# A perceiver layer on one core: outputs by transposes, values of four batches in one visit, and other steps of the cross-attention put elsewhere

## What is computed

```python
q = layernorm(x).reshape(B, 32, 16, 8)            # 16 heads of 8 channels
k = v = ctx.reshape(B, 257, 16, 8)
A = softmax(einsum('blhe,bshe->bhls', q, k) / sqrt(8)) * mask     # mask (32, 257)
out = einsum('bhls,bshd->blhd', A, v)
x = x + transpose(out, (0, 2, 1, 3)).reshape(B, 32, 128)   # heads first
```

## Time and profile before

| | us |
|---|---|
| runs: median of 3 (lowest to highest) | 1053.57 (1051.38 to 1054.31) |
| the profiled execution: its own time | 1050.45 |
| its span, first to last instruction | 1048.7 |
| stage 1: first scores to its last addition | about 20 to 529 |
| mean granted TensorE clock | 0.965 |

### The profile page before, as it was taken

How to read it: one execution, slowest core, us unless ns; L and a number is a source line. 1 busy time by engine, 2 the same in 40 slices (tenths; PEclk the granted TensorE clock), 3 DMA queues, 4 the chain that set the end, 5 groups by cost and what they waited for, 6 DMA issues and landing times. The chain is left out here.

```text
span 1048.7 us, 25999 instructions
## 1 busy us (share of the span) xinstructions
PE 927.9 (88%) x7666; PEld 815.4 (78%) x7666; DVE 840.0 (80%) x2152; ACT 648.9 (62%) x2006; POOL 606.9 (58%) x531
## 2 busy tenths in 40 slices
PE   3959999999999999999948888878899888888983
PEld 2848888888888888888848888778788787878872
DVE  5747787878788787878758887886499999999995
ACT  2626566656666566666536666666477777767674
POOL 4335555655555564556344444443477777877786
PEclk9979999999999999999969998999999999999997
DMA  4021212212221212221400000000000000000000
GB/s 119 25 74 56 58 50 65 55 47 60 55 65 43 65 55 52 56 65 54 142 1 1 0 0 0 0 0 1 1 2 10 5 10 5 10 5 6 9 5 16
DMA packets 48676, 35.34 MB, mean 34 GB/s; under 512 B 3660, under 2 KB 48392, under 8 KB 48648
## 3 DMA queue, kind: packets, MB, share of 16 engines
q1 hardware_dynamic: 48648, 35.00, 12.2%
HBM read 32.88 MB, written 2.10 MB: 33 GB/s over the span
## 5 line engine op out<-in xcount | busy, mean ns | idle before, releaser
L551 ACT ACTIVATE E<-SC,neg_max 128x257 f32<-128x257 f32 x512 | 238.4, 471 | 161.2 <-DVE neg_max L613 161.1
L425 PE MATMUL SC<-Kt,Qbd 128*128 128x257 f32 x1024 | 279.6, 396 | 1.0 <-ACT E L551 0.8
L613 DVE TENSOR_REDUCE neg_max<-SC 128x2 f32<-128x514 f32 x256 | 177.0, 691 | 86.6 <-PE SC L425 75.2
L425 PEld LDWEIGHTS SC<-Kt,Qbd 128*128 128x128 f32 x1024 | 176.9, 193 | 31.4 <-issue 14.1
L301 POOL TENSOR_TENSOR Qbd<-Qt,head_scaled 128x2048 f32<-128x2048 f32 (+2 forms) x33 | 145.1, 4398 | 80.0 <-ACT Qt L541 80.0
L621 DVE TENSOR_TENSOR Et<-ETP,mask_T 128x512 f32<-128x512 f32 x256 | 174.0, 680 | 15.0 <-PE ETP L439 14.9
L439 PE MATMUL ETP<-ident,E 128*128 128x128 f32 x1024 | 156.1, 275 | 0.0
L1371 PE MATMUL PO<-W,hid 128*128 128x128 f32 x1024 | 138.2, 278 | 18.8 <-ACT hid L1412 18.7
L1371 PEld LDWEIGHTS PO<-W,hid 128*128 128x128 f32 x1024 | 131.4, 192 | 29.0 <-issue 21.5
L1436 ACT ACTIVATE Y<-Z,zb,zs 128x128 f32<-128x128 f32 x256 | 111.0, 485 | 60.1 <-DVE zb L1591 60.1
L439 PEld LDWEIGHTS ETP<-ident,E 128*128 128x128 f32 x1024 | 125.3, 142 | 20.5 <-issue 0.4
(11 more groups left out here) (161 smaller groups left out, 1579.1 us busy)
## 6 DMA issues: line engine op xcount, KB each, us to landing
V<-in_ctx_dram SPq DMA_DIRECT2D x64, 256.0 KB, 2.9
last_all<-in_ctx_dram SPq DMA_DIRECT2D x32, 256.0 KB, 5.0
xh<-in_x_dram SPq DMA_DIRECT2D x32, 64.0 KB, 3.7
X<-in_x_dram SPq DMA_DIRECT2D x32, 64.0 KB
out_dram<-Xo SPq DMA_DIRECT2D x64, 32.0 KB, 1.5
W<-in_L_ffn_w_dram SPq DMA_DIRECT2D x1, 1024.0 KB
W<-in_L_ffn_w_dram SPq DMA_DIRECT2D x2, 512.0 KB
last_row<-in_ctx_dram SPq DMA_DIRECT2D x32, 2.0 KB
```

What stands on the lines that cost most here:

```text
L425: i = pe.matmul(SC[s % 2][:, u, 0:S], Qbd[:, h, jj, g:g + HQ, :].rearrange("p q l -> p (q l)"), Kt[:, h, jj, 0:S], start=True, stop=True)
L551: i = act.activation(E[:, h, u0 + u, :], SC[s % 2][:, u, 0:S], ACT.Exp, bias=neg_max[:, s % 2, u:u + 1], accum_out=den[:, h, u0 + u:u0 + u ...
L613: dve.tensor_reduce(neg_max[:, s % 2, :], SC[s % 2][:, :, 0:S], AX.X, ALU.max, negate=True).then_inc(max_sb, 1)
```

## The change

- The four products with `gather_d` become four transposes of `O_m` (128 columns a batch). The head mask falls away at `keep_sums`, which becomes a plain copy on ScalarE behind the exponentials of step 3 (`AV_STEP`). Shares are spread over heads instead (`spread_shares`, new, VectorE, step 3: reciprocal sums times the block mask, `own_p`), and `last_probs` and `own_outputs` multiply by them, 64 and 512 wide. GpSimd multiplies the last row by them in one instruction and then folds: three additions, 512, 256 and 128 wide (`fold` for `add_last`).
- `weigh_values` of four batches in one visit at step 2 of the next half; `Et` holds 16 steps instead of 8. The loads of the context follow: batches 4 and 5 of a tile are loaded with 6 and 7, 0 and 1 with 2 and 3.
- `turn_queries`, `keep_queries` and `place_last` at step 1 instead of 0.
- The second `turn_keys` at step 5 instead of 6 (`keep_keys` at 6), `turn_out` and `own_outputs` at step 4 instead of 5, `turn_tile` at 6 instead of 7.
- The tables are made within tile 0 (steps 3 to 6, in bank `AV`), the two memsets for stage 2 behind the first placing of queries there, and at the start some loads and small instructions change their order.

```diff
+AV_STEP = 3
...
 rden = sb1("rden", [P, HB * NQ])
-Et = sb1("Et", [P, HSTEPS, 2, KT, HQ * L])
+own_p = sb1("own_p", [P, HB * NQ, HQ])
...
+            load_ctx(sp, t, 2)
             load_ctx(sp, t, 3)
...
-        sp.wait_ge(av_ps, TB * t + 2)
-        sp.nop(nofuse=True)
-        load_ctx(sp, t + 1, 0)
...
+        load_ctx(sp, t + 1, 0)
         load_ctx(sp, t + 1, 1)
...
     load_x(sp, 0, 0)
     load_last(sp, 0, 0)
     load_ctx(sp, 0, 0)
+    load_x(sp, 0, 1)
+    load_ctx(sp, 0, 1)
+    load_last(sp, 0, 1)
     for n, src in zip("qkvo", (Wq, Wk, Wv, Wo)):
...
-    load_x(sp, 0, 1)
-    load_ctx(sp, 0, 1)
-    load_last(sp, 0, 1)
...
         m = 2 * t + h
         pool.wait_ge(all_in[h], 16 * (t + 1))
+        pool.wait_ge(p_last, m + 1)
         pool.tensor_tensor(last_x[:, :, :, :],
...
-    def add_last(t, h):
+                           last_p[:, :, :].unsqueeze(3).to_broadcast([P, HB * NQ, HQ, DK]),
+                           ALU.mult).then_inc(o_last, 1)
+
+    def fold(t, h):
 
         m, n = 2 * t + h, HB * NQ
         pool.wait_ge(o_n, m + 1)
         pool.wait_ge(o_last, m + 1)
-        mine = O_n[:, :, n * h:n * (h + 1)].rearrange("p d u -> p u d")
-        pool.tensor_tensor(mine, mine, last_o[:, :, :], ALU.add).then_inc(o_both, 1)
+        pool.tensor_tensor(last_x[:, :, :, :], last_x[:, :, :, :], own_x[:, :, :, :], ALU.add).then_inc(o_sum, 1)
+        pool.wait_ge(o_sum, m + 1)
+        pool.tensor_tensor(pair_x[:, :, :, :], last_x[:, :, 0:2, :], last_x[:, :, 2:4, :], ALU.add).then_inc(o_pair, 1)
+        pool.wait_ge(o_pair, m + 1)
+        if h == 0 and not (isinstance(t, int) and t == 0):
...
+        pool.tensor_tensor(O_n[:, :, n * h:n * (h + 1)].rearrange("p d u -> p u d"),
+                           pair_x[:, :, 0, :], pair_x[:, :, 1, :], ALU.add).then_inc(o_both, 1)
 
     def add_tile(t):
...
+            if fresh and h == 0:
+                pool.memset(Kbd[:, :, :, :], 0.0).then_inc(pool_set2, 1)
+                pool.memset(Vbd[:, :, :], 0.0).then_inc(pool_set2, 1)
             if h == 1 and not fresh:
...
 
     power(0, 0)
-    power(0, 1)
-    pool.wait_ge(dve_set, 1)
-    place_queries(0, 0, 0, 1, q_first)
-    place_queries(0, 0, 1, HB)
-
     pool.wait_ge(act_set2, 2)
     pool.affine_select(out=lag_ln[:, :], in_=lag_ln[:, :], compare_op=ALU.is_ge, fill=MASKED, base=0,
                        pattern=[[-1, L]], channel_multiplier=1).then_inc(pool_set2, 1)
...
+    place_queries(0, 0, 0, 1, q_first)
+    power(0, 1)
+    place_queries(0, 0, 1, HB)
+    pool.wait_ge(dve_set, 10)
...
-                              Et[:, 2 * (j % HB) + g // 2, g % 2, k, :],
+                              Et[:, 2 * j + g // 2, g % 2, k, :],
...
-            i = pe.matmul(MISC[:, 32 * j:32 * j + 32], O_m[:, j, :], gather_d[:, :, :].rearrange("p g d -> p (g d)"),
-                          start=True, stop=True)
+            i = pe.transpose(MISC[:, j * P:(j + 1) * P], O_m[:, j, :], ident[:, :])
...
-        if s % 4 == 3 and not (fresh and s < HSTEPS - 1):
-            tt, ss = back(t, s, 2 + 5)
-            weigh_values(tt, ss // 2, first=fresh and s < HSTEPS)
-            weigh_values(tt, ss // 2 + 1)
-        if s % HSTEPS == 5 and not (fresh and s < HSTEPS):
+        if s % HSTEPS == 2 and not (fresh and s < HSTEPS):
+            tt, ss = back(t, s, HSTEPS + 2)
+            for j in range(HB):
+                weigh_values(tt, ss // 2 + j, first=fresh)
+        if s % HSTEPS == 4 and not (fresh and s < HSTEPS):
             tt, ss = back(t, s, HSTEPS)
...
+
+    def tables(n):
+
+        if n == 0:
+            pe.wait_ge(dve_set2, 8)
+            pe.wait_ge(w2_in, 16 * 8)
+            pe.matmul(TAB_LAG, turn_l[:, :, :].rearrange("p q l -> p (q l)"), lag_p[:, :], start=True, stop=True)
+            pe.transpose(TAB_B, brow[:, :], ident[0:3, 0:3])
+            pe.wait_ge(b1_in, 16)
+            pe.transpose(TAB_B1, b1_rows[:, :], ident[0:NE * FH, 0:NE * FH]).then_inc(pe_set2, 1)
+        else:
+            pe.wait_ge(dve_set2, 11)
+            pe.matmul(TAB_OUT, bcol[:, 2:3].to_broadcast([P, P]), W["o"][:, :], start=True, stop=False)
...
     def steps(t, fresh, final):
         for s in range(STEPS):
             scores(t, s, first=fresh and s < 2)
-            if s == 0:
+            if s == 1:
                 turn_queries(t, 1)
-            if s == 8 and not final:
+            if s == 9 and not final:
                 turn_queries(t + 1, 0)
             if s % HSTEPS == 2:
                 turn_keys(t, 1 + 2 * (s // HSTEPS))
             lagging(t, s)
-            if s == 6:
+            if fresh and s in (3, 5):
+                tables(s // 2 - 1)
+            if fresh and s == 6:
+                pe.wait_ge(dve_set2, 12)
+            if s == 5:
                 turn_keys(t, 2)
-            if s == 14 and not final:
+            if s == 13 and not final:
                 turn_keys(t + 1, 0)
 
...
 
+    def keep_sums(t, h):
+
+        m = 2 * t + h
+        act.wait_ge(av_ps, HB * (m + 1))
+        if not (isinstance(t, int) and t == 0 and h == 0):
+            act.wait_ge(o_ps, m)
+        act.activation(O_m[:, :, :], AV[:, :, :], ACT.Copy).then_inc(o_m, 1)
...
     def steps(t, fresh, final):
         for s in range(STEPS):
-            if s % HSTEPS == 0 and not (final and s >= HSTEPS):
+            if s % HSTEPS == 1 and not (final and s >= HSTEPS):
                 keep_queries(t if s < HSTEPS else t + 1, 1 if s < HSTEPS else 0)
             if s % HSTEPS == 2:
                 keep_keys(t, 1 + 2 * (s // HSTEPS))
-            if s == 7:
+            if s == 6:
                 keep_keys(t, 2)
-            if s == 15 and not final:
+            if s == 14 and not final:
                 keep_keys(t + 1, 0)
             exponentials(t, s, first=fresh)
-
-    keep_queries(0, 0, first=True)
-    keep_keys(0, 0)
+            if s % HSTEPS == AV_STEP and not (fresh and s < HSTEPS):
+                keep_sums(*((t, 0) if s > HSTEPS else (t - 1, 1)))
...
     act.wait_ge(dve_set2, 2)
     act.activation(lag_ln[:, :], lag[:, :], ACT.Ln).then_inc(act_set2, 1)
     act.wait_ge(act_set2, 1)
     act.activation(lag_ln[:, :], lag_ln[:, :], ACT.Copy, scale=DECAY).then_inc(act_set2, 1)
+    keep_queries(0, 0, first=True)
+    keep_keys(0, 0)
...
-            dve.wait_ge(av_ps, TB * t + s // 2 - 3)
-        dve.tensor_tensor(Et[:, s % HSTEPS, :, :, :].rearrange("p u k c -> p (u k c)"), ETP[s % 2][:, :],
+            dve.wait_ge(av_ps, TB * t + HB if s >= STEPS - 2 else TB * (t - 1) + HB * (s // HSTEPS + 1))
+        dve.tensor_tensor(Et[:, s, :, :, :].rearrange("p u k c -> p (u k c)"), ETP[s % 2][:, :],
...
+    def spread_shares(t, h):
+        m = 2 * t + h
+        dve.wait_ge(rden_set, m + 1)
+        dve.tensor_tensor(own_p[:, :, :], rden[:, :].unsqueeze(2).to_broadcast([P, HB * NQ, HQ]),
+                          block_of[:, :].unsqueeze(1).to_broadcast([P, HB * NQ, HQ]), ALU.mult).then_inc(own_set, 1)
+
...
-        dve.wait_ge(rden_set, m + 1)
+        dve.wait_ge(own_set, m + 1)
         if not (isinstance(t, int) and t == 0 and h == 0):
...
-        dve.scalar_tensor_tensor(last_p[:, :], E[:, h, :, S - 1], mask_col[:, 0:1],
-                                 rden[:, :], ALU.mult, ALU.mult).then_inc(p_last, 1)
-
-    def keep_sums(t, h):
...
         dve.wait_ge(o_ps, m + 1)
-        dve.wait_ge(rden_set, m + 1)
-        if not (isinstance(t, int) and t == 0):
...
+        dve.wait_ge(own_set, m + 1)
+        if not (isinstance(t, int) and t == 0 and h == 0):
+            dve.wait_ge(o_sum, m)
+        dve.tensor_tensor(own_x[:, :, :, :], MISC[:, :].rearrange("p (u q d) -> p u q d", q=HQ, d=DK),
+                          own_p[:, :, :].unsqueeze(3).to_broadcast([P, HB * NQ, HQ, DK]), ALU.mult).then_inc(o_n, 1)
...
 
+    def tables(n):
+
+        dve.wait_ge(pe_set2, n + 1)
+        if n == 0:
+            dve.tensor_copy(decay[:, :, :], TAB_LAG.unsqueeze(1).to_broadcast([P, HB * NQ, L])).then_inc(dve_set2, 1)
+            dve.tensor_copy(bcol[:, :], TAB_B).then_inc(dve_set2, 1)
+            dve.tensor_copy(b1c[:, :], TAB_B1).then_inc(dve_set2, 1)
+        else:
+            dve.tensor_copy(out_bias[:, :], TAB_OUT).then_inc(dve_set2, 1)
+
...
+            if fresh and s in (4, 6):
+                tables(s // 2 - 2)
             if not final and s % HSTEPS == 4:
                 norm_stats(t + 1, s // HSTEPS)
             maxima(t, s, first=fresh and s < 2)
-            if s % HSTEPS == 4 and not (fresh and s < HSTEPS):
-                keep_sums(*((t, 0) if s > HSTEPS else (t - 1, 1)))
             if not final and s % HSTEPS == 4:
                 norm_mean(t + 1, s // HSTEPS)
             if not (fresh and s < 2):
                 tt, ss = back(t, s, 2)
-                keep_probs(tt, ss, first=fresh and s < HSTEPS + 2)
-            if s % HSTEPS == 0 and not (final and s >= HSTEPS):
+                keep_probs(tt, ss, first=fresh or (isinstance(tt, int) and tt == 0))
```

(23 more changed lines are left out.)

92 lines of the change are left out of this document (22 added, 70 removed).

## The result

The changed kernel takes 1072.83 us (median of 4 runs, 1070.31 to 1075.23), the kernel before 1052.47 in the same comparison (1050.59 to 1054.31): ratio 1.0207, 95% interval 1.0179 to 1.0235. It is slower by about 21 us, where 8.4 were forecast. The profiled execution took 1070.31 (span 1068.6), against 1050.45 (1048.7).

The account below looks back on a forecast made before the run. TensorE's own queue was taken to bound the changed stage, with thin margin behind it. Terms +22 - 11.5 + 0.5 - 7 + 1.6 + 0.8 + 2 = +8.4 gave 1058.9 or 1062.0, stated as 1060; range 1040 to 1076.

Parts of the forecast that it names:

- Rival 1: Steady halves: TensorE stays the bound, a half takes 14.3 + 0.27, total 1020; chance 0.13.
- Rival 3: Values visit: one visit costs as much as two, +0.39 in 31 halves, +12, total 1072; chance 0.11.
- the steady half: The 28 half tiles between step 11 of tiles 1 and 15: mean half 15.95 instead of 15.18, +22.
- the start: Tile 0, tables no longer ahead of it: scores of step 2 at 13.7 against 25.14, -11.5.
- the stall: Tile 1, VectorE waiting for x of tile 2: wait falls from 12.38 to about 5.5, -7 (bounds -3 and -12).
- the tail: End of the changed stage: three GpSimd additions after own_outputs where one stood, +2 (0.9 to 2.5); last half, +0.8.
- Rival 2: At turn_tile: only its wait is absent, 0.25 instead of 0.85 in 14 halves, -9, total 1051; chance 0.18.
- The reason within the half: Behind the visit: without ScalarE's 0.75 own_outputs would end at 5.25 all the same, and step 5's keys wait for it.
- the sum of 4.07: VectorE's back-to-back operations from 1.18 after the scores of step 3, adding to 4.07, so own_outputs ends at 5.25.
- One visit's own price: TensorE's values work per half: one visit of four batches 2.01 against 2.40 for two visits, -0.39.
- Rival 4: Tile 1: the stall stays whole, since it hangs on the same o_last, +7, total 1067; chance 0.07.
- Rival 5: TensorE: the clock falls as transposes replace matmuls, each half some 13 longer, over 1400 in all; chance 0.01.

Follow-up runs that it names:

- e7_twice: The changed kernel with the four transposes of the probabilities made twice in step 4 of each half after tile 0; 1071.77 us, ratio 1.0173.
- e1_turn7: The changed kernel with turn_tile put back from step 6 to step 7 on VectorE, nothing else; 1056.85 us, ratio 1.0068.
- e5_av2: As e1_turn7, with ScalarE copying O_m after the exponentials of step 2 instead of step 3; 1056.87 us, ratio 1.0046.
- e6_av2_keys6: As e5_av2, with keys of the even pairs back from step 5 to step 6; 1060.18 us, ratio 1.0068.
- e9_under: As e6_av2_keys6 with the residual's loads moved earlier, plus VectorE's small operations of steps 3 and 4 moved to step 2; 1030.54 us, ratio 0.9809.

## Why the prediction came out as it did

**The sign and the mechanism were right.** The forecast said that TensorE's work falls by 0.84 a half and the half rises all the same, since VectorE is back to back behind the one visit and own_outputs ends 5.25 after the scores of step 3; measured 5.19 (208.21, where the keys are let go, less 203.02). TensorE waiting for O_m, plain steps held by the exponentials (steps 6 and 7 take 2.88 together, 2.87 forecast) and VectorE waiting for the fold are all in the trace. Rival 1, TensorE the bound at 1020, fell: four more transposes a half were free (e7_twice). Rival 3's number, 1072, is the one that came nearest to the time measured, and its mechanism fell too (below): that is chance.

**What failed is the size of the steady half:** 15.95 was said, 16.24 measured, 28 times 0.29, 8 us of the 11.5 by which the spans and the sum differ. (The rest: 2.0 at the start and the stall, -1.1 at the tail, 2.8 behind the changed stage. The term itself was rounded up: 28 halves of 15.5 + 0.425 give +20.8, not +22.) Step by step, forecast and first half of the table: up to step 5 3.9 and 4.03; step 5 1.9 and 1.78; step 6 1.3 and 1.31; step 7 1.6 and 1.57; step 0 1.3 and 1.41; step 1 1.7 and 1.80; step 2 3.8 and 3.91. So the term was short by a tenth in four places (timeline, ScalarE and TensorE's weight load):

```profile
205.83 0.59 ACT L563 ACTIVATE O_m<-AV 128x512 f32<-128x512 f32 x1
...
214.87 0.73 PEld L420 LDWEIGHTS SC<-Kt,Qbd 128*128 128x128 f32 x4 [0.16 <-ACT E L553]
```

Up to step 5, the copy of O_m ended 3.40 behind the scores of step 3, as forecast (205.83 + 0.59 - 203.02), but the outputs behind it began at 3.54 (206.56). At step 0, scores that waited take 1.13 instead of 1.03 (211.67, and 213.07 for the next), and I had put this 0.10 behind the values alone. At step 1 the scores that follow wait 0.16 for exponentials, which the sum did not have. At step 2 the visit took 1.88 instead of 1.82. With turn_tile the difference of the two halves was 0.99 instead of 0.85: GpSimd's product and the first addition of the fold took 1.22 and 1.34 to the next start (191.21, 192.43, 193.77) where 1.12 and at most 1.2 were said. Rival 2 (no wait there) fell by e1_turn7, which took out just this.

**The reason within the half was half right.** That O_m sooner alone would bring nothing held, and so did the reason given: the keys then wait for own_outputs (0.63 in e5_av2). That this path sets the half did not: without that wait too the half stayed (e6_av2_keys6). The maxima of step 5, queued behind own_outputs on VectorE, and what hangs on them took its place; the sum of 4.07 ends with own_outputs, ahead of them, and the text did not name them.

**One visit's own price held.** 1.88 lie between the first value product and the scores (201.14 to 203.02); with 0.09 ahead of it and 0.10 in the next step that is 2.07, against 2.01 forecast and 2.40 for two visits. Rival 3 (as dear as two visits) fell; what the visit costs beside this is the idle time of the others.

**The start held, for this kernel:** scores of step 2 at 13.44, forecast 13.7. VectorE's normalise stood 3.42 beside GpSimd's placing of 3.40, as the order put it ahead of the first maxima (timeline, VectorE and GpSimd):

```profile
8.22 3.42 DVE L612 TENSOR_SCALAR xn<-xh,xmv,xrs 128x128 f32<-128x128 f32 x1 [1.10 <-POOL xrs L304]
...
8.15 3.40 POOL L297 TENSOR_TENSOR Qbd<-Qt,head_scaled 128x1536 f32<-128x1536 f32 x1
```

**The stall was mis-sized:** a wait of 5.5 was said, 8.44 measured; in TensorE's time 9.0 of 13.4 stayed, so 4.4 were won, not 7. x was issued at 50.97 and landed 7.2 later (58.19), longer than the 6.55 of before, though no load of V stood between. Rival 4 (the stall stays whole) was nearer than I thought.

**The tail** took 1.7 with the last half, of 2.8 forecast.

**Rival 5, the clock, fell:** the granted clock is 1.00 in the repeated stretch although the outputs are transposes too now, and 0.966 over the whole of the changed kernel (0.965 before). By the rule of the Trainium skill, "TensorE: Matmul & The Clock Gate", Part 4: PE-mode transpose, that transposes do not count as busy, it could have come; this trace, in which score passes stand between the transposes, does not bear it out.

**What no term had:** the stages behind, unchanged, took 2.8 longer in the changed kernel's profile. Over the fifteen profiled executions told of here they took from 519.7 to 525.3, without relation to the edit (span less the end of the last addition to X). This is why the halves, not the totals, carry the verdicts.

## What to carry to other kernels

Joining two visits of one engine saves on that engine only; ask how long its consumers run dry meanwhile, and what stands in their queues, in order, right behind it. When a wait is taken away and the time does not move, look for the next wait that came instead, and for a time that stays the same distance from a fixed event while the waits change (here 5.71 behind the scores of step 3). Such a time is a suspect, not a proof: the proof is to shorten that row and nothing else, as e9_under did. Small operations of a full row are best moved under the stretch in which their engine idles, and a run of DMA issues ahead of a load that is wanted soon is worth a look for an earlier gap in the queue.
